# 32-head attention with values and ones of 14 heads moving past turned probabilities, and a mixture's rows in expert order

## The reference, cut to what matters

```python
x = x + tanh(g_xattn[0]) * _L0_xattn_ref(_layernorm(x), ctx_1024, ...)      # 16 heads of 128
x = x + tanh(g_ffn[0])   * _L0_ffn_ref(_layernorm(x), gate_up, down)        # dense mixture, 4 experts
x = x + tanh(g_xattn[1]) * _L1_xattn_ref(_layernorm(x), ctx_1024, pos, ...) # 32 heads of 8
...                                                                         # five more parts
def _L0_ffn_ref(x, gate_up_proj, down_proj):
    x4 = x.reshape(B, G, E, H)                       # E = 4: token t to expert t % 4
    gu = einsum('bgeh,ehd->bged', x4, gate_up_proj)  # H = 256, 2 I = 512
    inter = silu(gu[..., :I]) * gu[..., I:]
    return einsum('bgei,eih->bgeh', inter, down_proj).reshape(B, N, H)
def _L1_xattn_ref(x, ctx, ...):
    q = rope(x @ Wq); k = rope((ctx @ Wkv)[k half]); v = (ctx @ Wkv)[v half]
    w = softmax(einsum('bqhd,bkhd->bhqk', q, k) / sqrt(8))
    return einsum('bhqk,bkhd->bqhd', w, v).reshape(b, n, 256) @ Wout + bout
```

## Time and profile before

| | |
|---|---|
| median of 3 runs | 2891.41 us (2885.76 to 2894.27) |
| profiled execution | 2908.03 us, span of its instructions 2906.3 us |
| busy, share of the span | PE 82%, PEld 50%, DVE 47%, ACT 42%, POOL 38% |
| mean granted TensorE clock | 0.905 of 2.4 GHz |
| dense mixture | 453.3 to 533.0 us |
| 32-head attention, first scores to last YT | 558.8 to 957.8 us |

### The profile page before, as it was taken

The page is one execution under the profiler, slowest core; times in us unless marked ns, Lnnn a source line. Parts: engine busy times, 40 slices in busy tenths (PEclk is TensorE's granted clock), DMA queues, the critical chain, the costliest instruction groups (busy, mean ns, idle before and its releaser), DMA issues.

```text
span 2906.3 us, 35500 instructions
## 1 busy us (share of the span) xinstructions
PE 2387.3 (82%) x10340; PEld 1458.7 (50%) x10340; DVE 1373.3 (47%) x3509; ACT 1212.1 (42%) x4398; POOL 1106.1 (38%) x1086
## 2 busy tenths in 40 slices
PE   5999999788899899989999997899948765713663
PEld 4666668544444344446665664466634333302553
DVE  2443343477777333345555543433367755830112
ACT  3444442365666221266665553233336553501111
POOL 3211110243444000034445352255524555446775
PEclk8999999999999999999999999999959877756777
DMA  9910000100000300000000003356541000003776
GB/s 347 350 61 1 1 1 1 40 1 1 1 1 1 107 1 0 1 1 1 1 1 32 3 29 107 117 96 102 94 128 63 8 8 1 8 8 71 151 150 143
DMA packets 159440, 162.72 MB, mean 56 GB/s; under 512 B 26931, under 2 KB 151107, under 8 KB 158484
## 3 DMA queue, kind: packets, MB, share of 16 engines
q1 hardware_dynamic: 127124, 119.64, 13.7%
q0 software_dynamic: 32128, 40.82, 7.9%
HBM read 81.35 MB, written 79.10 MB: 55 GB/s over the span
## 4 chain that ended last, share of the span: by engine, by line
issue 34%; PE 15%; DVE 6%; DMA 4%; POOL 4%; ACT 4%; another core or an unknown queue 2%; SPq 1%; POOLq 0%; DVEq 0%; ACTq 0%
PE ps L133 11%; DMA moe_sum<-work,weights 3%; ACT work L949 2%; POOL slots L2632 2%; POOL work L2709 1%; PE ps L884 1%; DMA work<-xn_rows,weights 1%; DVE n_mx L974 1%; PE ps L2070 1%; PE ps L2085 1%; POOL moe_sum L2723 1%; DVE xn L249 1%; DVE weights L2680 0%; ACT weights L2360 0%
## 5 line engine op out<-in xcount | busy, mean ns | idle before, releaser
L133 PE MATMUL ps<-work,weights 128*128 128x512 f32 (+4 forms) x2188 | 827.5, 547 | 36.0 <-issue 22.0
L133 PE MATMUL ps<-xn_T,weights 128*128 128x512 f32 (+5 forms) x1392 | 573.9, 552 | 26.1 <-DMA weights<-in_L_ffn_Wd 7.1
L133 PEld LDWEIGHTS ps<-work,weights 128*128 128x128 f32 (+3 forms) x2188 | 336.8, 199 | 274.7 <-issue 220.2
L949 ACT ACTIVATE work<-ps,n_negm 128x128 f32<-128x128 f32 (+2 forms) x1024 | 334.4, 358 | 215.6 <-DVE n_negm L977 215.2
L133 PE MATMUL ps<-weights,work 88*128 (+4 forms) x1472 | 398.7, 396 | 6.4 <-DVE weights L430 4.7
L133 PEld LDWEIGHTS ps<-xn_T,weights 128*128 128x128 f32 (+3 forms) x1392 | 254.3, 195 | 213.9 <-issue 180.6
L1031 POOL TENSOR_TENSOR work<-work,n_rinv 128x512 f32<-128x512 f32 (+2 forms) x256 | 215.9, 856 | 294.1 <-DVE n_rinv L983 293.1
L715 POOL TENSOR_TENSOR work<-work,rinv 128x512 f32<-128x512 f32 x128 | 133.5, 1043 | 307.4 <-DVE rinv L665 281.2
L133 PEld LDWEIGHTS ps<-weights,work 128*128 128x128 f32 (+2 forms) x1472 | 229.8, 197 | 40.9 <-issue 6.9
L949 ACT ACTIVATION_READ_ACCUMULATOR work<-ps,n_negm 128x1 f32 x1024 | 224.3, 223 | 0.0
L255 POOL TENSOR_TENSOR rstd<-var,neg_half 128x4 f32<-128x4 f32 x32 | 35.2, 1101 | 422.8 <-DVE var L240 422.8
(11 more groups left out here) (297 smaller groups left out, 3599.1 us busy)
## 6 DMA issues: line engine op xcount, KB each, us to landing
f_rows<-weights SPq DMA_DIRECT2D x17, 2176.0 KB, 19.5
weights<-in_L_ffn_gate_up_proj SPq DMA_DIRECT2D x16, 768.0 KB, 6.4
work<-f_rows SPq DMA_DIRECT2D x80, 136.0 KB
weights<-in_L_ffn_W SPq DMA_DIRECT2D x96, 88.0 KB
weights<-in_L_ffn_down_proj SPq DMA_DIRECT2D x16, 384.0 KB, 7.4
f_sum<-weights SPq DMA_DIRECT2D x2, 2176.0 KB, 15.1
moe_sum<-weights POOLq DMA_DIRECT2D x2, 2176.0 KB
weights<-in_L_xattn_Wo SPq DMA_DIRECT2D x2, 2048.0 KB, 12.4
```

What stands on the lines that cost most here:

```text
L133: return nc.tensor.matmul(out, lhsT, rhs, start=start, stop=stop, skip_group_check=True)
L949: last = nc.scalar.activation(n_p[:, i, j, lo:hi], S_BANKS[t % 3][:, j * P + lo:j * P + hi], ACT.Exp, bias=n_negm[:, i, m:m + 1], scale=sc ...
```

## The change

1. XNT of the stage before the mixture is written in expert order: tail_act permutes the columns of a body while it copies (for tails of stage 1), and ffn0_pe takes each expert's tokens as 128 contiguous columns.
2. The 32-head attention gets functions of its own (Slim). The turned probabilities of one head are stationary, and the values move past them. v_flat holds, for each head, 8 values and a one (9 columns); the matmul of head h moves the columns of heads h to h + 13 (126 of them) and writes them at column 9h of the output bank. Only the first 9 are head h's product and its sum of probabilities; the others are overwritten by the heads after it. So the output has tokens on partitions. After 8 units (a batch) DVE takes the reciprocals of the 32 sums, multiplies, PE turns the result with two transposes and ACT copies it. The sums are no longer accumulated by the Exps, POOL no longer multiplies, the head mask and the reduction over heads on DVE are gone.
3. Lags are one step shorter (transposes at t - 3, value product at t - 4), scores are issued behind transposes and value product of their step, and on DVE the copy of B6 stands behind maximum and negm. The tail begins at t = 10, the output product at t = 7.
4. The values are written by one activation for each half body instead of four, and their tile is set to 1.0 once.

```diff
     def tail_act(act, n, s, k):
         done(act, xn_tr, n, k)
-        nc.scalar.activation(XNT[:, k, tok(s)], TP, ACT.Copy).then_inc(xnt_ready.sem, 1)
+        if n // NS == 1:
+            nc.scalar.activation(XNT[:, k, tok(s)].rearrange("p (e t) -> p t e", e=E0), TP.rearrange("p (t e) -> p t e", e=E0),
+                                 ACT.Copy).then_inc(xnt_ready.sem, 1)
+        else:
+            nc.scalar.activation(XNT[:, k, tok(s)], TP, ACT.Copy).then_inc(xnt_ready.sem, 1)
...
-        xe = XNT.rearrange("p k (s t e) -> p k s e t", s=NS, e=E0)
...
-                        rhs = xe[:, k, bass.ds(s, 1), e, :].rearrange("p s t -> p (s t)")
+                        rhs = XNT[:, k, bass.ds(s * W + e * TE, TE)]
                         last = mm(bank[:, m * P:(m + 1) * P], l0_gu[:, e, k, m * P:(m + 1) * P], rhs, k == 0, k == KD - 1)
...
+            self.hd = D // heads
+            self.vw = self.hd + 1
+            self.wide = P // self.vw * self.vw
...
+    P_LAG = 3
+    PV_LAG = 4
+    NORM_LAG = 5
+    O_LAG = 6
+    OUT_AT = O_LAG + 1
+    def slim_out(blk):
+        return (B7, Y[1])[blk % 2]
+    def slim_pe(pe, S, q_t, v_flat, o_t, beside):
+        for t in S.steps:
+            u = t - P_LAG
+            if S.has(u):
+                done(pe, A.p_ready, s, u)
+                done(pe, A.pt_ready, s, u - 1)
+                for j in range(NB):
+                    last = nc.tensor.transpose(B6[:, j * P:(j + 1) * P], n_p[:, u % 4, j, :], ident[:])
+                last.then_inc(A.pt_tr.sem, 1)
+            u = t - PV_LAG
+            if S.has(u):
+                blk, g = u // A.groups, u % A.groups
+                done(pe, A.pt_ready, s, u)
+                if u in A.needs_v:
+                    done(pe, A.needs_v[u][0], s, A.needs_v[u][1])
+                if g == 0:
+                    done(pe, A.ot_ready, s, blk - 2)
+                    if blk == 1:
+                        done(pe, yt_ready, S.n, 1)
+                for j in range(NB):
+                    h = g * NB + j
+                    v0 = (blk % TB * A.heads + h) * A.vw
+                    last = mm(slim_out(blk)[:, h * A.vw:h * A.vw + A.wide], n_pt[:, u % 2, j * P:(j + 1) * P], v_flat[:, v0:v0 + A.wide])
+                last.then_inc(A.o_mm.sem, 1)
+            for g in (t, t + 1) if S.new and t % 2 == 0 else ():
+                c, r, b, hf = place(A, g)
+                r0 = r * A.rows
+                if g in A.needs_qk:
+                    done(pe, A.needs_qk[g][0], s, A.needs_qk[g][1])
+                if r == 0:
+                    done(pe, A.kblk_ready, s, c)
+                before = g - 3 if g >= 3 else max(i for i in range(A.n - 3, A.n) if i % 3 == g) - A.n
+                done(pe, A.p_ready, s, before)
+                mm(S_BANKS[g % 3], q_t[r0:r0 + A.rows, hf, b * P:(b + 1) * P],
+                   n_kblk[r0:r0 + A.rows, c % 2, :, :].rearrange("p h k -> p (h k)")).then_inc(A.s_mm.sem, 1)
+            u = t - O_LAG
+            blk = A.last_of(u)
+            if S.has(u) and blk is not None:
+                done(pe, A.on_ready, s, blk)
+                for hf in range(KD):
+                    last = nc.tensor.transpose(slim_out(blk)[:, hf * P:(hf + 1) * P], n_on[:, blk % 2, hf * P:(hf + 1) * P], ident[:])
+                last.then_inc(A.o_tr.sem, 1)
...
+        def turned(u):
+            blk = A.last_of(u)
+            if S.has(u) and blk is not None:
+                done(act, A.o_tr, s, blk)
+                if blk == 0:
+                    done(act, A.y_mm, s, -1)
+                b = blk % TB
+                nc.scalar.activation(o_t[:, :, b * P:(b + 1) * P], slim_out(blk)[:, 0:D].rearrange("p (k c) -> p k c", k=KD), ACT.Copy)\
+                    .then_inc(A.ot_ready.sem, 1)
+        for t in S.steps:
+            if S.old and t - OUT_AT in (1, 2):
+                out_of_y(S.n, t - OUT_AT - 1)
+            turned(t - O_LAG - 1)
+            u = t - P_LAG
+            if u % 2 == 0 and S.has(u):
+                done(act, A.pt_tr, s, u)
+                done(act, A.o_mm, s, u - 2)
+                nc.scalar.activation(n_pt[:, u % 2, :], B6, ACT.Copy).then_inc(A.pt_ready.sem, 1)
+            if S.new:
+                i = t % 4
+                done(act, A.negm_ready, s, t)
+                done(act, A.pt_tr, s, t - 4)
+                for j in range(NB):
+                    last = nc.scalar.activation(n_p[:, i, j, :], S_BANKS[t % 3][:, j * P:(j + 1) * P], ACT.Exp,
+                                                bias=n_negm[:, i, j:j + 1], scale=scale)
+                last.then_inc(A.p_ready.sem, 1)
...
+    def slim_dve(dve, S, scale, beside):
+        A, s = S.A, S.s
+        link = S.chain(dve, A.chain, 1, s)
+        for t in S.steps:
+            u = t - NORM_LAG
+            blk = A.last_of(u)
+            if S.has(u) and blk is not None:
+                o = slim_out(blk)[:, 0:A.heads * A.vw].rearrange("p (h d) -> p h d", d=A.vw)
+                done(dve, A.o_mm, s, u)
+                link(nc.vector.reciprocal(n_rinv, o[:, :, A.hd]))
+                done(dve, A.o_tr, s, blk - 2)
+                nc.vector.tensor_tensor(n_on[:, blk % 2, :].rearrange("p (h d) -> p h d", d=A.hd), o[:, :, 0:A.hd],
+                                        n_rinv.unsqueeze(2).broadcast_to([P, A.heads, A.hd]), ALU.mult).then_inc(A.on_ready.sem, 1)
+            if S.new:
+                done(dve, A.s_mm, s, t)
+                link(nc.vector.tensor_reduce(n_mx[:, t % 4, 0:NB], S_BANKS[t % 3].rearrange("p (h k) -> p h k", h=NB), AX.X, ALU.max))
+                done(dve, A.p_ready, s, t - 4)
+                nc.vector.tensor_scalar(n_negm[:, t % 4, 0:NB], n_mx[:, t % 4, 0:NB], -scale, None, ALU.mult)\
+                    .then_inc(A.negm_ready.sem, 1)
+            u = t - P_LAG
+            if u % 2 and S.has(u):
+                done(dve, A.pt_tr, s, u)
+                done(dve, A.o_mm, s, u - 2)
+                nc.vector.tensor_copy(n_pt[:, u % 2, :], B6).then_inc(A.pt_ready.sem, 1)
...
-    l1_v = tile(R1, 0, TB * KD * 4 * P).rearrange("p (t h r c) -> p t h r c", t=TB, h=KD, r=4)
+    l1_vw = L1HD + 1
+    l1_wide = P // l1_vw
+    l1_vf = tile(R1, 0, (TB * L1H + l1_wide - 1) * l1_vw)
+    l1_v = tile(R1, 0, TB * L1H * l1_vw).rearrange("p (t h d) -> p t h d", t=TB, h=L1H)
...
-    L1 = Narrow("a1", 2, L1H, P, l1_wout, l1_bias, 9)
+    L1 = Slim("a1", 2, L1H, l1_wout, l1_bias, 10)
...
-        v = TP.rearrange("p (t h r c) -> p t h r c", t=CB, h=KD, r=4)
-        for r in range(4):
-            c = slice(r * P // 4, (r + 1) * P // 4)
-            ins = nc.scalar.activation(l1_v[:, j * CB:(j + 1) * CB, :, r, c], v[:, :, :, r, :], ACT.Copy)
-        ins.then_inc(l1_v_ready.sem, 1)
+        nc.scalar.activation(l1_v[:, j * CB:(j + 1) * CB, :, 0:L1HD], TP.rearrange("p (t h d) -> p t h d", t=CB, h=L1H), ACT.Copy)\
...
-        nc.gpsimd.memset(l1_v, 0.0).then_inc(pool_consts, 1)
-        run_ahead(lambda S: narrow_pool(pool, S, l1_k, hmask8, nothing), L1, pool)
+        nc.gpsimd.memset(l1_vf, 1.0).then_inc(pool_consts, 1)
+        run_ahead(lambda S: slim_pool(pool, S, l1_k, hmask8), L1, pool)
...
```

More of the change, by code:

```diff
@@ L1036, in narrow_pool, with __init__, last_of @@
             beside(S, t)
+    class Slim:
+        def __init__(self, name, stage, heads, wout, bias, tail_t):
+            self.name, self.stage, self.heads, self.wout, self.bias = name, stage, heads, wout, bias
+            self.hd = D // heads
+            self.vw = self.hd + 1
+            self.wide = P // self.vw * self.vw
+            assert (heads - 1) * self.vw + self.wide <= W
+            self.rows = NB * self.hd
+            self.per_half = P // self.rows
+            self.groups = KD * self.per_half
+            self.n, self.late = TB * self.groups, O_LAG + 1
+            self.units = TB * KD
+            self.needs_qk, self.needs_v = {}, {}
+            self.tail_t = tail_t
+            n = self.n
+            self.chain = signal("attn_chain", n + TB)
+            self.kblk_ready = signal("narrow_kblk_ready", self.units)
+            self.s_mm = signal("attn_s_mm", n)
+            self.negm_ready = signal("attn_negm_ready", n)
+            self.p_ready = signal("attn_p_ready", n)
+            self.pt_tr = signal("attn_pt_tr", n)
+            self.pt_ready = signal("attn_pt_ready", n)
+            self.o_mm = signal("attn_o_mm", n)
+            self.on_ready = signal("slim_on_ready", TB)
+            self.o_tr = signal("slim_o_tr", TB)
+            self.ot_ready = signal("narrow_ot_ready", TB)
+            self.y_mm = signal("attn_y_mm", KD)
+        def last_of(self, u):
+            return u // self.groups if u % self.groups == self.groups - 1 else None
@@ new lines, in slim_act, with out_of_y @@
+    def slim_act(act, S, scale, o_t, beside):
+        A, s = S.A, S.s
+        def out_of_y(n, k):
+            done(act, yt_tr, n - 1, 1)
+            done(act, A.y_mm, s, k - KD)
+            g = A.stage // 2
```

(35 more changed lines are left out.)

38 lines of the change are left out of this document (32 added, 6 removed).

## The result

The kernel after takes 2942.5 us (median of four runs, 2939.8 to 2944.0), the kernel before in alternation with it 2891.0 us: ratio 1.0175, 95% interval 1.0158 to 1.0192. The change costs 51.5 us where 7 were forecast, and the time lies outside the range of 2876 to 2928.

| stretch, by the end of the bodies' last activation into YT | before, us | after, us | forecast of the difference | measured |
|---|---|---|---|---|
| mixture, four bodies | 80.3 | 58.1 | -21 | -22.2 |
| 32-head attention, four bodies and their drain | 422.7 | 494.7 | +28 | +72.0 |
| its second body | 100.4 | 119.4 | | +19.0 |
| its third body | 101.7 | 116.1 | | +14.4 |

What follows compares the result with a forecast made beforehand. TensorE (PE) was taken to bound both changed stages, the attention with gaps. Mixture -21 and attention +28 (413 against 399 at full clock, plus 14 for the clock) gave +7: 2898 us, range 2876 to 2928.

Steps and rivals of the forecast that it cites:

- Mixture (-21): First dense mixture: contiguous XNT cuts matmul time, body from 19.9 to 14.2 us; 21 us saved, bounds 17 and 28.9.
- rival (e): Mixture: XNT's stride was not the cause, the 21 us don't come, 2919 us; chance 0.05.
- The stall: Attention, each pair of steps: PE idles 1.75 us before transposes, waiting for DVE's copy of B6 behind maximum and negm.
- The rest of the pair: Attention, steady pair: scores 1.1, transposes to transposes 1.4, transposes 0.45, product 0.9; with the idle 1.75, 5.6 us.
- The clock (14 us): Attention: one half-clock spell per body stays after the norm stall, some 7 us, 3.5 lost each: +14.
- rival (c): Attention: 1.75 us gaps in each 5.6 lower the clock, pair 9.2; at 11 more pairs +40, 2938 us; chance 0.15.
- the main case: Whole kernel: mixture -21, attention +28, sum +7, 2898 us; spread -12 to +26 by its bounds; chance 0.60.
- Rival (b): Attention: without POOL and masks the pair falls to 4.3 us; with the mixture -83, 2808 us; chance 0.05.
- Rival (d): Attention value product: 126-column passes starting at multiples of nine cost 0.226 us like XNT's stride; +116, 3014 us; chance 0.05.
- Rival (a): Both ends good: mixture at its 28.9 bound, no clock loss in attention; -29 + 11 = -18, 2873 us; chance 0.10.
- The forecast of what is late next: Attention: ACT's copy of even u waits for Exp(t), put 0.4 us before needed; prediction fails if ACT is late.

## Why the prediction was right or wrong

**Mixture (-21): right.** Measured -22.2, body 14.2 to 14.9 against 14.2; that the last body stays at 14.9 hangs on the smaller tile for the values, which the prediction did not have in its sum. The stride was the cause, which refutes rival (e); the idle time before the y transposes is 0.99 us (1.1 forecast), before those of XN 0.29 (0.5). The copy into XNT in steps, priced at 1.05 us by YT's row, takes 1.06. The Trainium skill (SBUF — State Buffer, Door 1: The DMA port swizzle) asks for two hits in each 16-byte line. The traces agree with it: 0.226 us a pass on the stride, 0.112 without it.

**The stall (1.75 us, "a place in a queue"): right in place, releaser and size** (1.67 or 1.74 us in 29 waits of the stage, 1.92 in twelve), and shown by moving the copy. The rest of the pair was a little short, 5.8 to 5.9 us for 5.6: from transposes to transposes it is 1.72 us where ScalarE's copy is late, forecast 1.4; that copy stands behind the four Exps, which take 1.14 us together and not 0.8. PE in a pair of the second body:

```profile
683.70 0.63 PE L1104 MATMUL ps<-ident,work 128*128 128x128 f32 x4 [1.67 <-DVE work L1217]
684.16 1.05 PE L134 MATMUL ps<-weights,work 128*128 128x126 f32 x8
685.42 0.63 PE L1104 MATMUL ps<-ident,work 128*128 128x128 f32 x4 [0.21 <-ACT work L1178]
685.89 1.06 PE L134 MATMUL ps<-weights,work 128*128 128x126 f32 x8
```

The pair at the norm takes 10.3 us (701.82 to 712.16) with one spell in it and 9.0 without (the same pair in the kernel filled with transposes), so 3.2 more than usual for 2.5. Together a full-clock body is 108 to 109 us for the 104 forecast, and the stage 445 to 449 for 437 (the forecast 413 and the 23.7 us ahead of its stretch): 8 to 12 us of the miss.

**The clock (14 us): this step failed.** The sentence was "I expect one such spell for each body to stay". There are 7 and 5 in the two middle bodies and 28 in the stage; they cost 45 to 50 us, not 14: 31 to 36 us of the miss. The two parts make 44 us by either price, and 28 + 44 is the 72 measured. The step put the clock's loss in the gaps of the steady pairs at nothing; filling these gaps took away all spells but the two at the start of the stage. The mechanism was in the text as rival (c) with a chance of 0.15 and its place, the 1.75 us gaps. That its price, 2938 us, came close is luck: it is 11 pairs at 3.6 us more each, while some 25 pairs lost 1.5 us each. A steady pair never went to 9.2 us; spells come and go.

The evidence that misled was one row, 660 to 664 with PE busy for 2.36 of 4 us at clock 1.00. A single stretch showed that such a share can keep the clock once, not that it does so in each pair. In after, 664 to 668 is busy for 2.33 of 4 us and at 0.76. And the stretch of before moved 512 columns in its product passes, where after moves 126; the runs with 63 and 9 columns show that this matters. The Trainium skill (TensorE: Matmul & The Clock Gate, Part 4: PE-mode transpose), by which transposes do not count as PE-busy in the same way, pointed to rival (c). That was the right side for a reason that the runs do not bear out here: 13 transposes in the gap kept the clock as 12 matmul passes did.

Two sums of the text are off, without effect on the forecast: half clock for 12% of 399 us is 48 us and not 42 (the clock record of before has 44), and the bounds of the main case, taken at their ends, give -19 to +33 us and not -12 to +26.

**Rival (b)** (2808 us, "only if the copy is not behind the maximum") had the right picture and one condition too few: with that copy alone moved the ratio is 0.9936, 2873 us on the scale of the forecast's median. With both copies ahead the pair is 3.94 us and the ratio 0.9774, 2826 us. **Rival (d)** is refuted: passes of 126 columns take 0.11 us (eight in 0.89), though they start at every multiple of nine. **Rival (a)** had both ends wrong: the norm was shorter with POOL quieter (2.10 us for the four, 702.49, against 3.53 in the earlier trace rows), but the gaps elsewhere decided.

**The forecast of what is late next**, ScalarE's copy behind Exp(t), was right as a warning, not in its number: it was put 0.4 us early, is 0.21 us late in after, and 1.26 to 1.75 us in the kernel with only VectorE's copy moved.

## What to carry to other kernels

When work is taken off an engine, look at what stands in front of each short instruction that releases TensorE: two copies issued behind a maximum and an Exp group cost some 82 us of 445 here at full clock. With them moved, the stage is 32 us under that of before (422.7 - 0.485 x 58.0 = 395 against 363); with them in place, 50 over it. Price a periodic gap twice, once as idle time and once for the clock, and do not take one undisturbed stretch as proof that the clock holds. Here the gaps cost about 39 us through the clock, and filling them gave 32 back. When an instruction waits for a producer that stands late in its own queue, issuing the waiting one later moves only the wait; move the producer.

## What the runs showed of the hardware

- Passes of 9, 63 and 126 columns cost nearly the same at full clock (about 0.11 us), but with 63 or 9 the granted clock fell from 0.90 to 0.67 and 0.60 with gaps, and to 0.71 with 9 columns and no gaps. The kernels with passes of 126 columns, 117 of them thrown away, are 4 to 5% of the whole time faster than those with 9. Whether the moved columns themselves or something that goes with them decides, these runs do not show.
- Work that is thrown away, put into a 1.7 us gap, made the stage 32 us shorter.
- A matmul of two fp32 128x128 operands is two passes (13 of them 3.01 us, 724.15 to 727.16), a transpose of the same size one (13 of them 1.47 us, 725.61 to 727.08).
